# Router scores from a difference of logits on VectorE, one load of the first tokens, and eight fewer waits

## The chip, the cores and the metric

The kernel runs on one core of a Trainium2 chip. The core has five engines with a queue of instructions each: PE (TensorE, matmuls and transposes), DVE (VectorE), ACT (ScalarE), POOL (GpSimd) and SP (SyncE, which here only issues DMAs). Each engine works through its own queue in order and waits at semaphores for the others. The metric is device time in microseconds (us), the median over several executions.

## The reference

The block takes x of shape (4, 1024, 512), thus 4096 tokens of 512 channels. It normalises them with a scale and shift from a conditioning vector, applies a state-space layer of 16 states, adds that to x, normalises again, and adds a mixture of 8 experts. All experts are computed for every token; the router gives 2 of them a score and the other 6 zero.

```python
h = _layernorm(x) * (1 + ca) + sa
x = x + ga * attn(h)          # conv of 4 taps, projections, softplus, scan
h = _layernorm(x) * (1 + cb) + sb
x = x + gb * ffn(h)

# attn: h_t = deltaA_t * h_(t-1) + deltaBu_t, y_t = sum over 16 states of h_t * C_t
# ffn:
logits = jnp.tanh(xt @ Wg1.T) @ Wg2.T              # tokens x 8
_, top_idx = jax.lax.top_k(logits, 2)
top_scores = softmax(take_along_axis(logits, top_idx, axis=1), axis=1)
scores = zeros.at[rows, top_idx].set(top_scores)
up = einsum('td,ehd->teh', xt, Wup) + bup
down = einsum('teh,eoh->teo', silu(up), Wdown) + bdown
out = einsum('te,teo->to', scores, down)
```

With the two largest logits m0 >= m1 of a token, the two scores are 1/(1 + exp(m1 - m0)) and exp(m1 - m0)/(1 + exp(m1 - m0)).

## The kernel before

The 4096 tokens are cut into 8 chunks c of 512. Channels lie on the 128 partitions in 4 tiles. A chunk has 64 scan units (16 states times 4 channel tiles) of 128x512 elements, and each unit goes over four engines:

- ACT writes exp(delta * A) to PSUM (`da`, L996).
- POOL multiplies delta*u by a row of B (`dbu`, L796; DB <- DU, BR).
- DVE runs the scan (`scan`, L1210) into H.
- PE transposes H to tokens x channels in PSUM (`flip`, L1431), and DVE multiplies that by C and adds it to ACC (`acc`, L1235).

The expert layer works on half chunks cs of 256 tokens, 0 to 15. While chunk c is scanned, the two half chunks of chunk c-1 go through the router and the experts: PE multiplies upwards (`up`, L1480 to L1482), ACT applies tanh (`th`, L1098) and a multiply (`t1`, L1103), DVE multiplies by the token's score (`ys`, L1284), POOL makes the product G (`g`, L819), and PE multiplies downwards (`dn`, L1510). At the same time the attention part of the next chunk is prepared: convolution (`conv` on DVE, L1177; `cva` on POOL), projections, softplus, and at the end `del` and `du` on POOL (L760) and `ud` on ACT (L983).

The router of a half chunk is a chain of small steps. PE makes the logits; DVE copies them to LG (L1241), takes the 8 sorted maxima of both halves of 128 tokens into MX (`r3`, L1247) and their indices into IX (`r31`, L1254). ACT then makes PE1 = exp(MX1 - MX0) with one activation for each column (`e1`, L1060) and P0 = PE1 + 1 (L1063). DVE takes P1 = 1/P0 (`r41`, L1257) and P2 = PE1 * P1 (`r42`, L1261). POOL casts the indices from integers to floats, IXF (`r4`, L782), and spreads the two scores over the 8 experts (`sel1` and `sel2` in `select`, L537 to L549); for half chunks 14 and 15 DVE does the latter. PE transposes the result (`r5`, L1467), and through DRAM it comes back as the tile SR that `ys` reads. All steps on DVE here count one semaphore, rt.

The order of the work is written out by hand. `schedule()` makes one list of all tasks of all engines. Each scan unit has two places, numbered over a chunk from 0 to 127, and tables say at which place a task stands: ATTENTION, ROUTER (with a row for each kind of half chunk: "even", "odd", "final", "last", "split"), and PAIR and others for the experts. Each engine walks the list and issues the tasks that are its own. So a table sets only the order within each engine's queue, and semaphores do the rest. In ROUTER a half chunk of the kind "even" has its maxima at place 33 and the scores at 35 to 39 of a chunk, and one of the kind "odd" at 94 to 101.

At the start, SP issues the loads (`begin`, L558 to L567). The first chunk of x comes in two DMAs of 256 tokens, each with its own semaphore (d_xh, d_x). DVE takes the statistics (`sta`, L1166, L1168), POOL the scale (L712 to L718), ACT applies it (`xn`, L898), and PE transposes (`tr`, L1382) after it has made rows of the modulation (L1309). SP waits for the second half of the weight block WM0 (d_wmh) before it issues the loads of AN (A_log) and of WM2.

The weights of the upward product are split into a high part (`whi`, ACT L1018) and a low part (`wlo`, POOL L777, 16 instructions, during chunk 0). A `wlo` issued after the 12th convolution step waits for the convolution step that stands ahead of it in the list.

Of the kernel before, what the change touches and what calls it, by code (L numbers as in the profile page):

```python
# [65 lines left out]
             "r31": 33, "e1": 35, "r4": 38, "r41": 35, "r42": 38, "sel1": 39, "sel2": 39, "r5": 40,  # L66
# [3 lines left out]
             "r31": 96, "e1": 97, "r4": 100, "r41": 98, "r42": 99, "sel1": 101, "sel2": 101, "r5": 101,  # L70
# [3 lines left out]
             "r31": 96, "e1": 97, "r4": 99, "r41": 100, "r42": 100, "sel1": 103, "sel2": 103, "r5": 107,  # L74
# [3 lines left out]
             "r31": 66, "e1": 67, "r4": 69, "r41": 71, "r42": 74, "sel1": 70, "sel2": 76, "r5": 79,  # L78
# [3 lines left out]
             "r31": -18, "e1": -16, "r4": -16, "r41": -15, "r42": -14, "sel1": -14, "sel2": -14,  # L82
# [229 lines left out]
def adaln_kernel(nc, x, pvec, alog, ct, wmod, xpT, dtT, wg1T, wg2T, wupT, bup, wdT, bdn, out):  # L312
    f32, f32r, u32 = mybir.dt.float32, mybir.dt.float32r, mybir.dt.uint32
    ALU, ACT = mybir.AluOpType, mybir.ActivationFunctionType
    EPS = 1e-5
    ctx = ExitStack()
    with ctx:  # L317
# [209 lines left out]
        def select(eng, what, cs):  # L527

            if what == "sel1":
# [4 lines left out]
                eng.wait_ge(S["ixf"], cs + 1)  # L534
                eng.wait_ge(S["rt"], 6 * cs + 5)
# [3 lines left out]
            else:  # L539
                eng.wait_ge(S["rt"], 6 * cs + 6)  # L540
# [13 lines left out]
        def _(eng):  # L554
            for task in order:
                what, *k = task
                if what == "begin":
# [994 lines left out]
```

## Time and profile before

| | |
|---|---|
| Median of 3 runs | 1410.06 us (1409.54 to 1411.26) |
| The profiled execution | 1411.26 us, span of the records 1409.5 us |
| PE (matmul) busy | 1328.6 us, 94% of the span |
| DVE busy | 1222.1 us, 87% |
| POOL busy | 1138.8 us, 81% |
| ACT busy | 987.0 us, 70% |
| Reciprocals L1257 of half chunks 4 and 6 | start at 523.74 and 681.97 us |

A share is taken over the whole span. DVE, POOL and PE all come close to full use in parts of it, so which of them is waited for changes from place to place, and the shares alone don't tell it. A row of a timeline gives an instruction's start, its duration and, in brackets, how long its engine stood idle before it and what that idle time ended with. The time in which one and the same router step comes round again, 158.2 us, is the time of a chunk.

### The profile page before, as it was taken

Reading aid. Unit: us, or ns where it says so; the run is one execution under the profiler, and the core shown is the slowest. Engines: PE = TensorE matmul, PEld = TensorE weight load, DVE = VectorE, ACT = ScalarE, POOL = GpSimd, SP = SyncE. Lnnn points to the kernel's source line nnn. Section 1 sums busy time; section 2 is a strip of 40 time slices with the busy share of each in tenths; the row PEclk is TensorE's granted clock in tenths of the full one; section 3 lists DMA queues with packets and bytes.
Section 4 is the critical chain, followed back from the end, with each engine's and each line's share of the span. In section 5 each row is a group of like instructions: output and inputs, shape, how many; then the busy total and the mean of one; then the engine's idle time right before and its main releaser. Section 6 shows DMA issues by size and latency. Waiting matters only on the chain. (4 is left out here: it accounts for less than half of the span.)

```text
span 1409.5 us, 23418 instructions
## 1 busy us (share of the span) xinstructions
PE 1328.6 (94%) x7500; PEld 956.8 (68%) x7500; DVE 1222.1 (87%) x1725; ACT 987.0 (70%) x2076; POOL 1138.8 (81%) x1173
## 2 busy tenths in 40 slices
PE   8888768999999999999999999999999999999998
PEld 4466645667766776667766776767766767777897
DVE  4799999889897999889997999789998999897554
ACT  4875787588857796588857796588847675656554
POOL 1699889799996989899996989799996978873332
PEclk9899777999999999999999999999999999999999
DMA  6442112334242433534342433434332334433342
GB/s 207 165 151 62 60 38 89 97 96 150 88 136 83 150 120 101 140 97 150 93 132 89 147 117 104 139 94 150 98 131 87 127 105 118 131 90 106 128 134 65
DMA packets 99282, 160.91 MB, mean 114 GB/s; under 512 B 9276, under 2 KB 33980, under 8 KB 99160
## 3 DMA queue, kind: packets, MB, share of 16 engines
q1 hardware_dynamic: 99160, 159.42, 36.5%
q8 instruction: 60, 0.98, 0.3%
q14 instruction: 62, 0.51, 0.1%
HBM read 150.60 MB, written 8.79 MB: 113 GB/s over the span
## 5 line engine op out<-in xcount | busy, mean ns | idle before, releaser
L796 POOL TENSOR_TENSOR DB<-DU,BR 128x512 f32<-128x512 f32 x448 | 579.1, 1309 | 44.7 <-DVE H L1210 23.2
L1235 DVE SCALAR_TENSOR_TENSOR ACC<-pb,CTM,ACC 128x512 f32<-128x512 f32 x512 | 374.9, 733 | 56.0 <-PE pb L1431 54.7
L1510 PE MATMUL pb<-WD,G 128*128 128x512 f32 x856 | 405.1, 593 | 0.0
L996 ACT ACTIVATE pb<-DELP,AN 128x512 f32<-128x512 f32 x448 | 307.2, 686 | 133.5 <-DVE H L1210 131.4
L1431 PEld LDWEIGHTS pb<-ID,H 128*128 128x128 f32 x2048 | 246.9, 144 | 147.8 <-issue 97.6
L1431 PE MATMUL pb<-ID,H 128*128 128x128 f32 x2048 | 316.3, 281 | 26.1 <-DVE ACC L1235 22.0
L1480 PE MATMUL pb<-H2H,WUH 128*128 128x256 f32 x1024 | 314.1, 307 | 13.4 <-DVE TY L1284 12.9
L1210 DVE TENSOR_TENSOR_SCAN H<-pb,DB 128x512 f32<-128x512 f32 x256 | 309.9, 1212 | 15.1 <-ACT pb L996 12.1
L819 POOL TENSOR_TENSOR G<-TY 128x256 f32<-128x256 f32 x256 | 192.0, 753 | 145.2 <-DVE TY L1284 101.2
L1482 PE MATMUL pb<-H2H,WUL 128*128 128x256 f32 x1024 | 289.7, 283 | 0.0
L1481 PE MATMUL pb<-H2L,WUH 128*128 128x256 f32 x1024 | 289.5, 283 | 0.0
L1210 DVE TENSOR_TENSOR_SCAN H<-pb,ST,DB 128x512 f32<-128x512 f32 x192 | 244.4, 1273 | 8.5 <-ACT pb L996 6.6
L1510 PEld LDWEIGHTS pb<-WD,G 128*128 128x128 f32 x856 | 149.0, 190 | 111.9 <-issue 111.0
L1480 PEld LDWEIGHTS pb<-H2H,WUH 128*128 128x128 f32 x1024 | 195.5, 191 | 37.6 <-issue 25.6
L1481 PEld LDWEIGHTS pb<-H2L,WUH 128*128 128x128 f32 x1024 | 196.1, 192 | 4.8 <-issue 4.3
L1482 PEld LDWEIGHTS pb<-H2H,WUL 128*128 128x128 f32 x1024 | 195.5, 191 | 0.0
L1098 ACT ACTIVATE TY<-pb,BUPH 128x256 f32<-128x256 f32 x256 | 106.8, 468 | 123.5 <-PE pb L1482 120.9
L1284 DVE SCALAR_TENSOR_TENSOR TY<-pb,BUP,SR 128x256 f32<-128x256 f32 x256 | 111.1, 474 | 38.5 <-ACT TY L1098 29.8
L1103 ACT ACTIVATE TY<-TY 128x256 f32<-128x256 f32 x256 | 102.5, 413 | 0.0
L1215 DVE TENSOR_TENSOR_SCAN H<-pb,ST,DB 128x256 f32<-128x256 f32 x128 | 88.4, 732 | 2.6 <-ACT pb L1001 1.9
L799 POOL TENSOR_TENSOR DB<-DU,BR 128x512 f32<-128x512 f32 x64 | 81.7, 1287 | 1.7 <-DVE H L1215 1.6
L1332 PE MATMUL pb<-H2H 128*128 128x256 f32 x292 | 58.6, 333 | 3.2 <-ACT H2H L846 3.2
(199 smaller groups left out, 1681.3 us busy)
## 6 DMA issues: line engine op xcount, KB each, us to landing
WD<-in_wdT SPq DMA_DIRECT2D x128, 512.0 KB, 5.0
BR<-bscr SPq DMA_DIRECT2D x112, 256.0 KB, 3.9
SR<-sscr SPq DMA_DIRECT2D x128, 128.0 KB, 4.2
ACC<-in_x SPq DMA_DIRECT2D x16, 512.0 KB, 3.8
out<-ACC SPq DMA_DIRECT2D x32, 256.0 KB, 2.2
DU<-in_x SPq DMA_DIRECT2D x7, 1024.0 KB, 6.5
BR<-bscr SPq DMA_DIRECT2D x32, 128.0 KB, 3.1
DU<-in_xpT SPq DMA_DIRECT2D x8, 320.0 KB, 3.1
```

The lines of the kernel that those rows point to most:

```text
L796: eng.tensor_tensor(DB[:, i % NDB], DU[:, c % 2, r], BR[:, n % 2], ALU.mult).then_inc(S["dbu"], 1)
L819: eng.tensor_tensor(G[:, i % NG], TH[:, m % 2], YS[:, m % 2], ALU.mult).then_inc(S["g"], 1)
L996: eng.activation(DA[i % NDA][:], DEL[:, c % 2, r], ACT.Exp, scale=AN[:, r, n:n + 1]).then_inc(S["da"], 1)
L1098: eng.activation(TH[:, m % 2], up_of(cs, m), ACT.Tanh, scale=0.5, bias=BUPH[:, m:m + 1]).then_inc(S["th"], 1)
L1210: eng.tensor_tensor_scan(H[:, (c * NS + n) % NH, r], DA[i % NDA][:], DB[:, i % NDB], ST[:, n, r:r + 1] if state_from(c, h) else 0.0, ALU.mult,
L1235: eng.scalar_tensor_tensor(out=acc, in0=banks[bank_of["flip", c, n, r]][:], scalar=1.0 if n < 0 else CTM[:, c % 2, j, st:st + 1], in1=acc, ...
L1284: eng.scalar_tensor_tensor(out=YS[:, m % 2], in0=up_of(cs, m), scalar=BUP[:, m:m + 1], in1=SR[:, m // 2 % 2], op0=ALU.add, op1=ALU.mult).t ...
L1431: t = eng.transpose(b[:, dt * 128:dt * 128 + 128], src[:, dt, r * 128:r * 128 + 128], ID[:])
L1480: eng.matmul(b, WUH[:, kk, sl], H2H[:, cs % 2, kk], start=kk == 0, stop=False)
L1481: eng.matmul(b, WUH[:, kk, sl], H2L[:, cs % 2, kk], start=False, stop=False)
L1482: t = eng.matmul(b, WUL[:, kk, sl], H2H[:, cs % 2, kk], start=False, stop=kk == 3)
L1510: eng.matmul(DN[j][:], G[:, (cs * NM + m) % NG, j * 128:j * 128 + 128], WD[:, (cs * NE + m // 2) % NWD, m % 2], start=False, stop=m == NM ...
```

## The change

It has three parts.

1. The router. DVE now makes DM = MX1 - MX0 (a new instruction, ahead of the indices), and ACT one exponential of both columns of DM where it made two, and no copy. DVE adds 1 (the new task `r40`, a tensor_scalar) and takes the reciprocal in place. The cast of the indices moves from POOL to DVE, and the table ROUTER puts it right behind the indices. The semaphores p0 and ixf are gone; rt counts 9 steps for each half chunk instead of 6.
2. The first loads. The first chunk of x comes in one DMA of 1 MB, and the statistics wait for all of it. SP no longer waits for d_wmh before the loads of AN and WM2.
3. The low part of the weights. The `wlo` tasks on POOL no longer wait for the convolution.

In numbers of instructions: DVE has 48 more (3 for each of 16 half chunks), ACT 32 fewer, POOL 16 fewer, SP one DMA fewer; 7 waits of `wlo` go. PE's are the same, in the same order.

```diff
 ROUTER = {
     "even": {...
-             "r31": 33, "e1": 35, "r4": 38, "r41": 35, "r42": 38, ...
+             "r31": 33, "e1": 35, "r4": 33, "r40": 34, "r41": 35, "r42": 38, ...
...
-        PE1, P0, P1, P2 = [RS[:, i] for i in range(4)]
+        DM, PE1, P1, P2 = [RS[:, i] for i in range(4)]
...                                                   # select, sel1
-                eng.wait_ge(S["ixf"], cs + 1)
-                eng.wait_ge(S["rt"], 6 * cs + 5)
+                eng.wait_ge(S["rt"], 9 * cs + 8)
...                                                   # SP, begin
-                    eng.dma_start(DU[:, 0, 0:2], x_v[0][:, 0:2]).then_inc(S["d_xh"], 16)
-                    eng.dma_start(DU[:, 0, 2:4], x_v[0][:, 2:4]).then_inc(S["d_x"], 16)
+                    eng.dma_start(DU[:, 0], x_v[0]).then_inc(S["d_x"], 16)
...
-                    eng.wait_ge(S["d_wmh"], 16)
...                                                   # POOL
-                    taps = [nth[t] for t in order[:at[task]] if t[0] == "conv"]
-                    if taps and taps[-1] > 12:
-                        eng.wait_ge(S["conv"], taps[-1])
...
-                elif what == "r4":
-                    cs = k[0]
-                    eng.wait_ge(S["rt"], 6 * cs + 4)
-                    eng.tensor_copy(IXF[:], IX[:]).then_inc(S["ixf"], 1)
...                                                   # ACT
-                    eng.wait_ge(S["rt"], 6 * cs + 2)
-                    for j in range(2):
-                        eng.activation(PE1[:, j:j + 1], MX[:, j, 0:1], ACT.Exp, scale=-1.0,
-                                       bias=MX[:, j, 1:2]).then_inc(S["e1"], 1)
-                    eng.wait_ge(S["e1"], 2 * (cs + 1))
-                    eng.activation(P0, PE1, ACT.Copy, bias=1.0).then_inc(S["p0"], 1)
+                    eng.wait_ge(S["rt"], 9 * cs + 3)
+                    eng.activation(PE1, DM, ACT.Exp).then_inc(S["e1"], 1)
...                                                   # DVE, sta of chunk 0
-                    if j % 2 == 0:
-                        eng.wait_ge(S["d_x" if j else "d_xh"], 16)
+                    if j == 0:
+                        eng.wait_ge(S["d_x"], 16)
...                                                   # DVE, router
-                    eng.wait_ge(S["rt"], 6 * cs + 2)
-                    if cs:
-                        eng.wait_ge(S["ixf"], cs)
+                    eng.wait_ge(S["rt"], 9 * cs + 2)
+                    eng.tensor_tensor(DM, MX[:, :, 1], MX[:, :, 0], ALU.subtract).then_inc(S["rt"], 1)
                     for j in range(2):
                         eng.max_index(IX[:, j], MX[:, j], LG[:, j]).then_inc(S["rt"], 1)
+                elif what == "r4":
+                    cs = k[0]
+                    eng.wait_ge(S["rt"], 9 * cs + 5)
+                    eng.tensor_copy(IXF[:], IX[:]).then_inc(S["rt"], 1)
+                elif what == "r40":
+                    cs = k[0]
+                    eng.wait_ge(S["e1"], cs + 1)
+                    eng.tensor_scalar(P1, PE1, 1.0, None, ALU.add).then_inc(S["rt"], 1)
                 elif what == "r41":
-                    eng.wait_ge(S["p0"], k[0] + 1)
-                    eng.reciprocal(P1, P0).then_inc(S["rt"], 1)
+                    eng.wait_ge(S["rt"], 9 * k[0] + 7)
+                    eng.reciprocal(P1, P1).then_inc(S["rt"], 1)
```

On DVE, around the maxima of half chunk 0 (kind "even"), this stands in a row before. `H<-pb,ST,DB` is a scan, `ACC<-pb,CTM,ACC` an `acc`; MX, IX, IXF and RS are the router's tiles, and RS holds DM, PE1, P1 and P2.

```order
L1235 SCALAR_TENSOR_TENSOR ACC<-pb2,CTM,ACC 128x512
L1247 MAX MX<-LG 128x8 x2
L1254 MAX_INDEX IX<-MX,LG 128x8 x2
L1210 SCALAR_TENSOR_TENSOR H<-pb1,ST,DB 128x512
L1235 SCALAR_TENSOR_TENSOR ACC<-pb4,CTM,ACC 128x512
L1257 RECIPROCAL RS<-RS 128x2
L1210 SCALAR_TENSOR_TENSOR H<-pb0,ST,DB 128x512
```

And now, in the same place:

```order
L1221 SCALAR_TENSOR_TENSOR ACC<-pb2,CTM,ACC 128x512
L1233 MAX MX<-LG 128x8 x2
L1237 TENSOR_TENSOR RS<-MX 128x2
L1239 MAX_INDEX IX<-MX,LG 128x8 x2
L1243 CAST IXF<-IX 128x16
L1196 SCALAR_TENSOR_TENSOR H<-pb1,ST,DB 128x512
L1247 TENSOR_SCALAR RS<-RS 128x2
L1221 SCALAR_TENSOR_TENSOR ACC<-pb4,CTM,ACC 128x512
L1250 RECIPROCAL RS<-RS 128x2
L1196 SCALAR_TENSOR_TENSOR H<-pb0,ST,DB 128x512
```

The difference and the cast stand ahead of the next scan, and the addition between that scan and the next `acc`.

On DVE, at the indices of half chunk 1 (kind "odd"), before:

```order
L1254 MAX_INDEX IX<-MX,LG 128x8 x2
L1235 SCALAR_TENSOR_TENSOR ACC<-pb3,CTM,ACC 128x512
L1210 SCALAR_TENSOR_TENSOR H<-pb1,ST,DB 128x512
L1257 RECIPROCAL RS<-RS 128x2
L1235 SCALAR_TENSOR_TENSOR ACC<-pb3,CTM,ACC 128x512
L1261 TENSOR_TENSOR RS<-RS 128x2
```

And now:

```order
L1237 TENSOR_TENSOR RS<-MX 128x2
L1239 MAX_INDEX IX<-MX,LG 128x8 x2
L1243 CAST IXF<-IX 128x16
L1221 SCALAR_TENSOR_TENSOR ACC<-pb3,CTM,ACC 128x512
L1196 SCALAR_TENSOR_TENSOR H<-pb1,ST,DB 128x512
L1247 TENSOR_SCALAR RS<-RS 128x2
L1250 RECIPROCAL RS<-RS 128x2
L1221 SCALAR_TENSOR_TENSOR ACC<-pb3,CTM,ACC 128x512
L1254 TENSOR_TENSOR RS<-RS 128x2
```

Here one `acc` and one scan stand between the cast and the addition, and the reciprocal follows the addition at once.

## Rows read from the trace of the kernel before

**Rows 1.** Three stretches: length, busy PE, PEld, DVE, ACT, POOL, clock, DMA, GB/s.

```profile
50.00:225.00 175.00, 135.95 (x752) 100.00 (x752) 167.93 (x196) 135.22 (x246) 157.65 (x144) 0.83 0.26 81
575.00:750.00 175.00, 171.94 (x971) 121.00 (x970) 155.66 (x210) 123.22 (x257) 154.10 (x158) 1.00 0.39 120
1290.00:1409.00 119.00, 110.87 (x690) 97.70 (x688) 64.11 (x114) 65.33 (x163) 41.81 (x49) 0.99 0.32 104
```

**Rows 2.** Timeline of DVE near 32 us: start, duration, instruction, times, idle before it.

```profile
32.62 0.18 DVE L1113 TENSOR_TENSOR MOD<-H 128x16 f32<-128x16 f32 x1
```

**Rows 3.** Timeline of DVE near 53 us.

```profile
52.04 1.19 DVE L1111 TENSOR_SCALAR GBC<-GBC 128x16 f32<-128x16 f32 x1
53.27 1.20 DVE L1113 TENSOR_TENSOR GBC<-GBC 128x16 f32<-128x16 f32 x1
```

**Rows 4.** Timeline of POOL in the same stretch (three instructions, printed as one row).

```profile
50.70 3.73 POOL L796 TENSOR_TENSOR DB<-DU,BR 128x512 f32<-128x512 f32 x3
```

**Rows 5.** Timeline of DVE near 521 us, half chunk 4.

```profile
521.31 0.22 DVE L1247 MAX8 MX<-LG 128x8 f32<-128x8 f32 x2
...
521.86 1.26 DVE L1210 TENSOR_TENSOR_SCAN H<-pb,ST,DB 128x512 f32<-128x512 f32 x1
```

**Rows 6.** Timeline of POOL in the same stretch.

```profile
521.17 0.74 POOL L819 TENSOR_TENSOR G<-TY 128x256 f32<-128x256 f32 x1
521.96 2.52 POOL L767 TENSOR_TENSOR H2L<-XT,H2H 128x512 fp32r<-128x512 f32 x2
```

**Rows 7.** Timeline of ACT near 606 us, half chunk 5.

```profile
605.84 0.47 ACT L1060 ACTIVATE RS<-MX 128x1 f32<-128x1 f32 x2
```

**Rows 8.** Timeline of DVE in the same stretch.

```profile
603.81 0.75 DVE L1235 SCALAR_TENSOR_TENSOR ACC<-pb,CTM,ACC 128x512 f32<-128x512 f32 x1
...
606.58 0.17 DVE L1257 RECIPROCAL RS<-RS 128x2 f32<-128x2 f32 x1 [0.83 <-ACT RS L1063]
```

**Rows 9.** Timeline of POOL in the same stretch.

```profile
604.05 0.73 POOL L819 TENSOR_TENSOR G<-TY 128x256 f32<-128x256 f32 x1
...
606.96 1.43 POOL L537 TENSOR_SCALAR S<-IO,IXF,RS 128x104 f32<-128x104 f32 x2 [0.80 <-DVE RS L1257]
```

**Rows 10.** Timeline of DVE from 684 to 702 us, the rows with idle time.

```profile
686.14 1.22 DVE L1210 TENSOR_TENSOR_SCAN H<-pb,DB 128x512 f32<-128x512 f32 x1 [0.26 <-ACT pb L996]
...
690.98 0.75 DVE L1235 SCALAR_TENSOR_TENSOR ACC<-pb,CTM,ACC 128x512 f32<-128x512 f32 x1 [0.39 <-PE pb L1431]
...
697.39 1.23 DVE L1210 TENSOR_TENSOR_SCAN H<-pb,DB 128x512 f32<-128x512 f32 x1 [0.68 <-POOL DB L796]
```

**Rows 11.** Timeline of DVE from 529 to 540 us, the rows with idle time.

```profile
532.75 0.75 DVE L1235 SCALAR_TENSOR_TENSOR ACC<-pb,CTM,ACC 128x512 f32<-128x512 f32 x1 [0.37 <-PE pb L1431]
...
539.07 1.28 DVE L1210 TENSOR_TENSOR_SCAN H<-pb,ST,DB 128x512 f32<-128x512 f32 x1 [0.56 <-issue]
```

**Rows 12.** Timeline of DVE near 622 us.

```profile
622.50 1.28 DVE L1210 TENSOR_TENSOR_SCAN H<-pb,ST,DB 128x512 f32<-128x512 f32 x1 [2.11 <-ACT pb L996]
```

**Rows 13.** Timeline of PE near 625 us.

```profile
625.35 0.35 PE L1480 MATMUL pb<-H2H,WUH 128*128 128x256 f32 x1 [1.45 <-DVE TY L1284]
```

**Rows 14.** Timeline of PE near 211 us.

```profile
210.75 1.34 PE L1431 MATMUL pb<-ID,H 128*128 128x128 f32 x8 [1.38 <-DVE ACC L1235]
```

**Rows 15.** Timeline of POOL near 95 us.

```profile
94.62 1.26 POOL L777 TENSOR_TENSOR WUL<-XT,WUH 128x512 fp32r<-128x512 f32 x1 [0.69 <-DVE U L1177]
```

**Rows 16.** Timeline of DVE near 5 us.

```profile
5.34 0.69 DVE L1166 BATCH_NORM_STATS2 NA<-DU 128x6 f32<-128x512 f32 x1 [2.18 <-DMA DU<-in_x]
```

**Rows 17.** DMA issues of x, median us from issue to landing.

```profile
DU<-in_x SPq DMA_DIRECT2D x7, 1024.0 KB, 6.5
...
DU<-in_x SPq DMA_DIRECT2D x2, 512.0 KB, 4.6
```

**Rows 18.** Timeline of ACT near 11 us.

```profile
10.80 2.92 ACT L898 ACTIVATE DU<-DU,NA 128x512 f32<-128x512 f32 x4 [1.43 <-POOL NA L718]
```

**Rows 19.** Timeline of PE near 17 us.

```profile
16.59 0.66 PE L1382 MATMUL pb<-ID,DU 128*128 128x128 f32 x4
```

More of the change, by code:

```diff
@@ L65 @@
              "fev": (21, 25), "hh": 32, "hl": (35, 35), "r1": 26, "r12": 29, "r2": 28, "r22": 31, "r3": 33,
-             "r31": 33, "e1": 35, "r4": 38, "r41": 35, "r42": 38, "sel1": 39, "sel2": 39, "r5": 40,
+             "r31": 33, "e1": 35, "r4": 33, "r40": 34, "r41": 35, "r42": 38, "sel1": 39, "sel2": 39, "r5": 40,
              "r52": 43, "sw": 43},
@@ L69 @@
              "fev": (48, 52), "hh": 61, "hl": (65, 74), "r1": 82, "r12": 84, "r2": 89, "r22": 91, "r3": 94,
-             "r31": 96, "e1": 97, "r4": 100, "r41": 98, "r42": 99, "sel1": 101, "sel2": 101, "r5": 101,
+             "r31": 96, "e1": 97, "r4": 96, "r40": 98, "r41": 98, "r42": 99, "sel1": 101, "sel2": 101, "r5": 101,
              "r52": 104, "sw": 104},
@@ L73 @@
              "fev": (46, 49), "hh": 58, "hl": (57, 70), "r1": 81, "r12": 86, "r2": 89, "r22": 84, "r3": 96,
-             "r31": 96, "e1": 97, "r4": 99, "r41": 100, "r42": 100, "sel1": 103, "sel2": 103, "r5": 107,
+             "r31": 96, "e1": 97, "r4": 98, "r40": 100, "r41": 100, "r42": 100, "sel1": 103, "sel2": 103, "r5": 107,
              "r52": 106, "sw": 106},
@@ L77 @@
              "fev": (47, 50), "hh": 55, "hl": (52, 60), "r1": 55, "r12": 56, "r2": 60, "r22": 61, "r3": 66,
-             "r31": 66, "e1": 67, "r4": 69, "r41": 71, "r42": 74, "sel1": 70, "sel2": 76, "r5": 79,
+             "r31": 66, "e1": 67, "r4": 69, "r40": 69, "r41": 71, "r42": 74, "sel1": 70, "sel2": 76, "r5": 79,
              "r52": 79, "sw": 79},
@@ L81 @@
              "fev": (-34, -30), "hh": -23, "hl": (-25, -22), "r1": -24, "r12": -23, "r2": -20, "r22": -20, "r3": -19,
-             "r31": -18, "e1": -16, "r4": -16, "r41": -15, "r42": -14, "sel1": -14, "sel2": -14,
+             "r31": -18, "e1": -16, "r4": -17, "r40": -15, "r41": -15, "r42": -14, "sel1": -14, "sel2": -14,
              "r5": -9, "r52": -10, "sw": -8}}
@@ L435, in adaln_kernel @@
                      "du", "ud", "ug", "da", "dbu", "scan", "st", "flip", "acc", "asm", "ang", "asq", "fsm", "fng", "fsq", "frs", "fxn", "ftr", "fev",
-                     "hh", "hl", "g1", "tg", "g2", "lg", "rt", "sel", "bdz", "bdh", "bdl", "e1", "p0", "ixf", "r5", "stt", "up", "th", "ys", "t1", "g", "bm",
+                     "hh", "hl", "g1", "tg", "g2", "lg", "rt", "sel", "bdz", "bdh", "bdl", "e1", "r5", "stt", "up", "th", "ys", "t1", "g", "bm",
                      "dn0", "dn1", "to", "fin",
-                     "wh", "wl", "gh", "gl", "d_ctx", "d_x", "d_pv", "d_alog", "d_wm0", "d_wmh", "d_xh", "d_wm1", "d_wm2", "d_wm3", "d_wm4", "d_wm5", "d_wg1",
+                     "wh", "wl", "gh", "gl", "d_ctx", "d_x", "d_pv", "d_alog", "d_wm0", "d_wmh", "d_wm1", "d_wm2", "d_wm3", "d_wm4", "d_wm5", "d_wg1",
                      "d_wg2", "d_bup", "d_bdn", "d_xa0", "d_xa1", "d_xp", "d_dtp", "d_bw", "d_br0", "d_br1", "d_gs",
@@ L539, in select @@
             else:
-                eng.wait_ge(S["rt"], 6 * cs + 6)
+                eng.wait_ge(S["rt"], 9 * cs + 9)
                 for j in range(2):
@@ L1249, in _ @@
                     cs = k[0]
-                    eng.wait_ge(S["rt"], 6 * cs + 2)
-                    if cs:
-                        eng.wait_ge(S["ixf"], cs)
+                    eng.wait_ge(S["rt"], 9 * cs + 2)
+                    eng.tensor_tensor(DM, MX[:, :, 1], MX[:, :, 0], ALU.subtract).then_inc(S["rt"], 1)
                     for j in range(2):
                         eng.max_index(IX[:, j], MX[:, j], LG[:, j]).then_inc(S["rt"], 1)
+                elif what == "r4":
[6 more added lines that the diff above has]
+                    eng.tensor_scalar(P1, PE1, 1.0, None, ALU.add).then_inc(S["rt"], 1)
                 elif what == "r41":
-                    eng.wait_ge(S["p0"], k[0] + 1)
-                    eng.reciprocal(P1, P0).then_inc(S["rt"], 1)
+                    eng.wait_ge(S["rt"], 9 * k[0] + 7)
+                    eng.reciprocal(P1, P1).then_inc(S["rt"], 1)
                 elif what == "r42":
                     cs = k[0]
-                    eng.wait_ge(S["rt"], 6 * cs + 5)
+                    eng.wait_ge(S["rt"], 9 * cs + 8)
                     eng.tensor_tensor(P2, PE1, P1, ALU.mult).then_inc(S["rt"], 1)
```

## The prediction

> **What bounds the kernel now.** I read the busy times by stretch first. In a middle stretch of 175 us PE is busy for 171.94, DVE for 155.66 and POOL for 154.10 at a full granted clock; in 50 to 225 us DVE leads with 167.93 and PE has 135.95; in the last 119 us DVE is down to about half [rows 1]. So early in the kernel a microsecond more on DVE counts in full, in the middle PE sets the pace and a late DVE counts where its own idle gaps don't make it up, and at the end it hardly counts.
>
> Then the timelines at the router. After a router step of the even kind DVE has small gaps: in one pattern (half chunks 2, 6, 10) 0.26, 0.39 and 0.68 us [rows 10], in the other (4, 8) 0.37 and 0.56 us [rows 11]. In the odd kind the router is itself on the path. DVE stands 0.83 us before the reciprocal, for ACT's addition [rows 8]; six such waits, of half chunks 1 to 11, repeat this one; POOL stands 0.80 us for that reciprocal before it can spread the scores [rows 9]. Behind that POOL works without a gap to the products `du` of the next chunk, ACT waits for those, DVE then stands 2.11 us for ACT's exponential [rows 12], and PE 1.45 us for DVE's `ys` [rows 13]. That is the one place of a middle chunk at which PE, the bound, stands long; what moves the odd reciprocal moves it.
>
> **The router on DVE: what one small instruction costs.** Three are added for each half chunk. With POOL idle, an instruction of this size takes 0.18 us [rows 2], and starts follow each other at about 0.21: 48 of them would be 10 us of DVE, 0.63 for a half chunk. But the same chain of instructions, run a second time while POOL does its 128x512 products, took 1.19 for a tensor_scalar and 1.20 for a tensor_tensor on 16 columns [rows 3], and each ended where one of POOL's three products, 1.24 apiece, ended [rows 4]. So such a small one is held until the running POOL instruction is over. The maxima and indices are not held: beside POOL's G and H2L [rows 6], max and both indices are through in 0.55, from 521.31 to the scan at 521.86 [rows 5]. No row shows an integer cast on DVE beside POOL. Its bounds are 0.18 [rows 2] and the whole of one POOL product, 1.26 [rows 6]. I take the long one, since the nearest row in form (one input, one output, both in SBUF) is the tensor_scalar of 1.19 [rows 3]; the other end stays for the range.
>
> The Trainium skill bears on this value ("SBUF — State Buffer", section "Who interferes with whom"): copy, cast and tensor_scalar between SBUF tiles can run in modes that take the port pair shared with GpSimd, which is locked for a whole instruction by whoever comes first, and a tensor_tensor with two SBUF inputs contends with a GpSimd instruction that reads SBUF. The trace agrees for the two forms that it shows, 1.19 and 1.20 [rows 3]; by the rule the cast is held too, and by the unheld value instead the sum below would fall to the second rival's.
>
> **Even kind.** Laid on the timeline of half chunk 4: max ends at 521.53. The difference is held until G ends at 521.91, so it costs 0.4 instead of 0.2. The indices take 0.3, to 522.25. The cast is held to the end of the first of the two H2L products, 521.96 + 1.26 = 523.22 [rows 6]. The scan starts at 523.25, not 521.86 [rows 5]: +1.4. The addition stands behind this scan; ACT's exponential is long ready, and the scan ends near the end of the second H2L (524.48 [rows 6]), so I take it at 0.15 (bounds: 0.15 and 1.2, the tensor_scalar of [rows 3]). Together DVE is 1.55 late. In half chunk 0 the same laying gives 1.3 + 0.15 = 1.45.
>
> What becomes of it: half chunk 0 lies where PE waits for DVE at once, 1.38 us [rows 14], so all 1.45 count. In 2, 6 and 10 the gaps of [rows 10] give 1.33 back, leaving 0.22 each, 0.66. In 4 and 8 those of [rows 11] give 0.93 back, leaving 0.62 each, 1.24. Half chunk 12 and later ones I take at nothing: DVE is half idle there [rows 1]. Even kind: 1.45 + 0.66 + 1.24 = 3.35 us.
>
> **Odd kind.** Half chunk 5: the `acc` at 603.81 [rows 8] followed the indices, which take 0.3, so these began at 603.5. The difference is now there and held until POOL's product before G ends, at 604.05 [rows 9]; indices to 604.4; the cast is held to the end of G, 604.05 + 0.73 = 604.78 [rows 9]. An `acc` of 0.75 and a scan of 1.28 [rows 11] end at 606.8, the addition at 607.0, and the reciprocal begins there instead of at 606.58 [rows 8]: +0.4. ACT is no longer waited for: one exponential of the two that took 0.47 together [rows 7] ends near 606.1. So the wait of 0.83 goes, and DVE's own queue, held twice, is late in its place. Behind the reciprocal stand P2 and POOL's scores, and by the chain above the 0.4 goes on to PE. 6 such half chunks (1 to 11): 2.4 us. Half chunk 13 and the last: nothing.
>
> **Relief.** ACT loses one exponential and one copy for each half chunk, some 0.43 us. ACT is busy for 123.22 of 175 us [rows 1] and mostly waits for the scans, so I take nothing. POOL loses the cast, but stood waiting right behind it in the odd kind [rows 9]: nothing. The indices' wait for the cast of the half chunk before was long fulfilled.
>
> **The waits of `wlo`.** Only one was waited out: POOL stood 0.69 us for the convolution [rows 15], in a stretch where DVE needs POOL's products soon after. I take -0.3, between -0.7 (all of it) and +1.3 (that POOL product now starts beside the convolution and holds it once more, by one product of 1.26 as in [rows 15]).
>
> **The first loads.** DVE's statistics begin at 5.34, when the first half of x is there [rows 16]. A half took 4.6 us to land in the median, a whole chunk in later places 6.5 [rows 17]; so they begin up to 1.9 later. ACT's normalisation then ends at 13.72 + 1.9 = 15.6 [rows 18], and PE takes it up at 16.59 [rows 19], behind rows of the modulation. Cost 0, cover left 1.0 us. AN and WM2 are issued earlier behind the same loads and are not waited for early: 0 (bounds 0 and, if they slow the loads that PE waits for, +1).
>
> **Sum.** 3.35 + 2.4 - 0.3 = +5.45. The profiled execution took 1411.26 us (span 1409.5, 1.8 around it), so it becomes 1416.7; it stood 1.2 above the median, 1410.06, so the median becomes **1415.5**. Differences within 0.2%, 2.8 us, can't be told from no change.
>
> **Rivals.**
> 1. The lateness isn't given back. DVE's gaps [rows 10, 11] may only move with the work, because they end on PE and POOL, which DVE itself made late. Then the even kind costs 1.45 + 5 x 1.55 = 9.2, the odd 2.4: +11.3, 1421.4; with the addition held in some, 1423. For it: in 50 to 225 us DVE has 7 us to spare [rows 1]; against: the middle chunks are PE's. Chance 0.12.
> 2. The cast and the additions are not held, or only where it doesn't matter. 0.63 for a half chunk disappears in the gaps of 0.93 to 1.33, half chunk 0 costs 0.6, and the odd reciprocal comes at 603.81 [rows 8] + 0.42 + 0.75 + 1.28 + 0.2 = 606.5, 0.1 early: 0.6 - 0.6 - 0.3, so 1409.8. For it: no row shows the cast itself. Chance 0.25.
> 3. Faster. The holds fall short, and the odd chain, ACT to DVE to POOL to ACT to PE, shortens. The exponential is ready at 606.1 instead of the sum at 606.55, so 0.45 is the most that a reciprocal can come earlier: 6 x 0.45 + 0.7 of `wlo` + 0.3 of ACT in half chunk 0 = -3.7, 1406.4. It decides from where the difference and cast together cost DVE under 0.5 us in the odd kind, since DVE had 0.83 to spare [rows 8]. For it: that slack; against: [rows 3]. Chance 0.16.
> 4. The granted clock, 0.83 in the mean of 50 to 225 [rows 1], stays low for longer since PE has still more gaps there: 4 to 8 us more at half clock where PE is full cost 2 to 4 more, 1417.5 to 1419.5. With the first loads reaching the path, chance 0.05.
>
> The forecast itself has 0.42. Its own range is 1412.9 to 1418.5. Leaving out most of rival 3 (0.12) and the far part of rival 1 (0.07) gives 1408.0 to 1423.0. Faster is rival 3, 0.16; same is rival 2, 0.25; slower is the rest, 0.59.
>
> **What would show it.** Right: the cast lasts about 1 us in the even kind and 0.4 in the odd, the difference 0.4 to 0.6; the scan behind the even indices comes 1.4 later after max; no idle before the odd reciprocals, and POOL's wait for them at about 1.2; a chunk of about 159 us; first statistics near 6.7 to 7.2 with `tr` still near 16.6. Wrong: casts of 0.2 beside POOL products (rival 2); odd reciprocals earlier against their scans (rival 3); gaps behind the even kind as large as before and a chunk of 160 us (rival 1); a low clock past 230 us (rival 4).

## The result and the profile after

The changed kernel is slower. Its median is 1421.76 us over 6 runs (1417.25 to 1424.52); the kernel before took 1411.05 us in the same comparison (6 runs, 1409.54 to 1412.31). The ratio is 1.0075, with a 95% interval of 1.0056 to 1.0094, or 10.7 us. I had forecast +5.5 us, a time of 1415.5 and a range of 1408.0 to 1423.0. The direction and the mechanism (small DVE instructions held by POOL's products) were right, and the forecast size was half of what was measured. The single runs of the changed kernel lie 7.3 us apart, those of the kernel before 2.8.

The profiled execution of the changed kernel took 1423.32 us (span 1421.5), so it is one of its slower ones: 12.1 us above the profiled execution before.

The same stretches as in [rows 1], of the changed kernel. The columns are length, busy PE, PEld, DVE, ACT and POOL, clock, DMA share and GB/s:

```profile
50.00:225.00 175.00, 136.66 (x748) 99.27 (x748) 169.15 (x195) 130.40 (x238) 153.65 (x141) 0.83 0.24 78
575.00:750.00 175.00, 171.73 (x967) 120.47 (x966) 159.18 (x216) 121.36 (x249) 156.60 (x157) 1.00 0.40 123
1290.00:1409.00 119.00, 116.51 (x747) 103.84 (x746) 72.98 (x133) 70.11 (x175) 40.62 (x48) 1.00 0.37 113
```

In the middle stretch PE is as busy as before and DVE has 3.5 us more; the last stretch is shifted by 13 us against the work and compares with nothing. These rows tell little of the loss. The router's own instructions tell more. On the timelines the columns are start, duration, instruction, times and idle time before it. DVE at half chunk 4, where before max, indices and the scan followed each other within 0.55 us [rows 5]:

```profile
524.14 0.23 DVE L1233 MAX8 MX<-LG 128x8 f32<-128x8 f32 x2
524.40 0.35 DVE L1237 TENSOR_TENSOR RS<-MX 128x2 f32<-128x2 f32 x1
...
525.07 1.03 DVE L1243 CAST IXF<-IX 128x16 f32<-128x16 uint32 x1
526.02 1.27 DVE L1196 TENSOR_TENSOR_SCAN H<-pb,ST,DB 128x512 f32<-128x512 f32 x1
527.21 0.14 DVE L1247 TENSOR_SCALAR RS<-RS 128x2 f32<-128x2 f32 x1
```

The difference (L1237) takes 0.35 us, the cast (L1243) 1.03, and the scan starts 1.88 after max instead of 0.55: +1.33. The addition (L1247) takes 0.14. Half chunk 5 on DVE and on POOL, for [rows 8] and [rows 9]:

```profile
606.26 0.57 DVE L1237 TENSOR_TENSOR RS<-MX 128x2 f32<-128x2 f32 x1
...
607.15 0.38 DVE L1243 CAST IXF<-IX 128x16 f32<-128x16 uint32 x1
...
609.47 0.17 DVE L1250 RECIPROCAL RS<-RS 128x2 f32<-128x2 f32 x1
```

```profile
605.53 1.28 POOL L786 TENSOR_TENSOR DB<-DU,BR 128x512 f32<-128x512 f32 x1
606.76 0.74 POOL L809 TENSOR_TENSOR G<-TY 128x256 f32<-128x256 f32 x1
...
609.81 0.73 POOL L536 TENSOR_SCALAR S<-IO,IXF,RS 128x104 f32<-128x104 f32 x1 [1.08 <-DVE RS L1250]
```

The difference ends with POOL's product (606.83 and 606.81), and the cast about with G (607.53 and 607.50). The reciprocal no longer waits, and POOL waits 1.08 us for it where it waited 0.80.

To see where lateness comes and stays I took each PE matmul's start in one trace minus the start of the same matmul before (they stand in the same order in both). Columns are places on the time axis of the kernel before; half chunk 0 lies between 155 and 240 us, 2 to 8 up to 900, 12 between 1140 and 1190, 13 up to 1215, 14 up to 1275. Each row is one execution, with its time in the last column (before: 1411.26).

| kernel | 155 | 240 | 345 | 820 | 900 | 1140 | 1190 | 1215 | 1275 | 1400 | time |
|---|---|---|---|---|---|---|---|---|---|---|---|
| changed | 1.7 | 3.7 | 2.7 | 3.1 | 4.7 | 4.9 | 7.3 | 11.1 | 13.2 | 13.2 | 1423.32 |
| router alone | 0.1 | 0.9 | 0.3 | 1.3 | 2.8 | 3.0 | 5.4 | 5.6 | 7.6 | 7.6 | 1417.79 |
| old router from 12 on | 0.0 | 2.4 | 1.6 | 1.7 | 3.2 | 3.2 | 2.6 | 2.6 | 2.6 | 2.5 | 1412.71 |
| 19 waits on POOL | 1.8 | 3.1 | 3.4 | 7.0 | 7.3 | 9.7 | 9.3 | 9.3 | 10.2 | 10.2 | 1420.43 |
| 13 waits on POOL | 1.1 | 2.3 | 1.4 | 1.5 | 1.8 | 2.2 | 2.1 | 2.1 | 3.1 | 3.1 | 1413.35 |
| no difference on DVE | 3.4 | 5.9 | 4.9 | 4.6 | 5.0 | 5.0 | 7.4 | 7.6 | 9.0 | 9.0 | 1419.18 |
| old router, no `wlo` waits | 1.9 | 2.9 | 1.9 | 1.6 | 1.6 | 1.3 | 1.5 | 1.5 | 1.4 | 1.4 | 1411.71 |

(The step of -1 us between 240 and 345 is in most rows, also of kernels without the new router, so it belongs to the execution before. The changed kernel's last DMA wait was 1.1 us shorter, which is why 13.2 became 12.1.)

So of 13.2 us, 8.3 come in half chunks 12 to 14, which I had put at nothing, 2.0 in half chunk 0, and 1.7 before that, in chunk 0. The first columns are within what executions differ: seven of the kernels below run the same instructions and waits as the kernel before up to the first router step near 208 us, and their profiles lie -0.1 to 3.4 us late at 155. DVE and POOL at half chunk 13 of the changed kernel:

```profile
1202.53 0.21 DVE L1233 MAX8 MX<-LG 128x8 f32<-128x8 f32 x2
1202.77 3.58 DVE L1237 TENSOR_TENSOR RS<-MX 128x2 f32<-128x2 f32 x1
...
1209.93 1.11 DVE L1243 CAST IXF<-IX 128x16 f32<-128x16 uint32 x1
```

```profile
1202.55 2.55 POOL L789 TENSOR_TENSOR DB<-DU,BR 128x512 f32<-128x512 f32 x2
1205.05 1.28 POOL L814 TENSOR_TENSOR ACC<-ACC,XT 128x512 f32<-128x512 f32 x1
```

The difference of 2 columns takes 3.58 us. It waits out three of POOL's products, 1202.55 to 1206.33, not one. That happened in three of the five profiles of this and the later kernels that have the difference and no wait of POOL ahead of it (3.55 to 3.58 us); in the other two it took 1.09. PE before and after at half chunk 12, and after at 13:

```profile
1165.00 0.43 PE L1467 MATMUL pb<-ID,S 128*104 128x128 f32 x2 [1.07 <-POOL S L549]
```

```profile
1171.02 0.43 PE L1460 MATMUL pb<-ID,S 128*104 128x128 f32 x2 [2.21 <-POOL S L548]
```

```profile
1209.41 0.39 PE L1473 MATMUL pb<-H2H,WUH 128*128 128x256 f32 x1 [1.41 <-DVE TY L1277]
```

PE stood for POOL's scores there even before, 1.07 us, so what the router loses goes straight to PE: now 2.21. The clock adds to it. These are the stretches after the two gaps, first before and then after:

```profile
1165.00:1185.00 20.00, 19.58 (x116) 13.90 (x117) 17.77 (x30) 14.22 (x36) 15.08 (x15) 1.00 0.45 126
1200.00:1220.00 20.00, 20.00 (x119) 14.74 (x117) 17.85 (x32) 11.36 (x30) 18.22 (x23) 1.00 0.46 131
```

```profile
1165.00:1185.00 20.00, 17.62 (x98) 13.38 (x97) 19.35 (x33) 13.37 (x35) 15.74 (x19) 0.91 0.34 98
1200.00:1220.00 20.00, 18.28 (x99) 13.33 (x98) 19.33 (x35) 7.96 (x22) 15.00 (x16) 0.91 0.45 133
```

The granted clock is 0.91 in the mean there instead of 1.00: in each of the two, 3.4 us were granted at half, from 1172.5 and from 1210.1 us on (0.09 x 20 us is 1.8 us short of full speed, within rounding half of 3.4). Before, none was from 230 us to the last 3 us. By that the two cost at most 3.4 us of matmul time, an estimate: half of 3.4 us each.

And the convolution step near 91 us, before and after:

```profile
91.53 2.95 DVE L1177 SCALAR_TENSOR_TENSOR U<-DELP,PV,U 128x512 f32<-128x512 f32 x1
```

```profile
90.77 6.11 DVE L1163 SCALAR_TENSOR_TENSOR U<-DELP,PV,U 128x512 f32<-128x512 f32 x1
```

```profile
87.65 3.78 POOL L786 TENSOR_TENSOR DB<-DU,BR 128x512 f32<-128x512 f32 x3
91.38 1.29 POOL L771 TENSOR_TENSOR WUL<-XT,WUH 128x512 fp32r<-128x512 f32 x1
...
96.96 1.26 POOL L740 TENSOR_TENSOR U<-U,DU 128x512 f32<-128x512 f32 x1 [0.63 <-DVE U L1163]
```

Free it takes 0.72 us. Before, it was held until POOL came to the `wlo` that waited for it [rows 15]; in this execution, without that wait, it was held through five products, until POOL stood for it at L740.

### The profile page after: what moved, and what is told of

Read it like the earlier page. It is cut to its first block and busy times, and to the rows that moved or that the text cites. A ratio compares the mean times of both kernels' runs of the same rounds, so it can differ in the third digit from the quotient of the medians.

```text
span 1421.5 us, 23395 instructions
## 1 busy us (share of the span) xinstructions
PE 1335.9 (94%) x7500; PEld 959.8 (68%) x7500; DVE 1251.3 (88%) x1773; ACT 979.0 (69%) x2044; POOL 1135.9 (80%) x1157
## 5 line engine op out<-in xcount | busy, mean ns | idle before, releaser
L1163 DVE SCALAR_TENSOR_TENSOR U<-DELP,PV,U 128x512 f32<-128x512 f32 x57 | 63.2, 1116 | 2.0 <-ACT U L910 1.8
```

## The experiments

Each kernel was timed in 5 rounds against the kernel before; ratios are given with their 95% intervals. The theory (the port): a small DVE instruction is held while POOL's products run, and that lateness reaches PE. Rivals stand with each run.

**The waits of `wlo` put back.** The changed kernel with

```diff
+                    taps = [nth[t] for t in order[:at[task]] if t[0] == "conv"]
+                    if taps and taps[-1] > 12:
+                        eng.wait_ge(S["conv"], taps[-1])
```

> The changed kernel with the seven waits of wlo for the convolution put back; all else as changed. Theory P (the port): the convolution step that took 6.11 us near 91 us is held as long as POOL runs one product behind the other, and POOL's wait for it was what let it in, so with the waits it takes about 2.95 again and 1.7 us of the 10.7 go (what is left of that lateness at 140 us): about 1.0065 times the kernel before. Rival C (the clock): the early lateness comes from half-clock stretches that fell elsewhere, and the waits are worth nothing or the 0.3 us that I forecast: 1.0075 or a little above, with a convolution step as long as now.

Measured: 1419.23 us (6 runs, 1413.60 to 1423.15), ratio 1.0063 (1.0046 to 1.0080). The convolution step took 3.66 us. That goes with the theory, but the interval overlaps with that of the changed kernel (1.0056 to 1.0094), so on the time the run decides nothing. (The 1.7 us that the expectation puts at 140 us stand in the table at 155.)

**The waits of `wlo` taken away alone.** The kernel before without those three lines.

> The kernel before with only the seven waits of wlo taken away. Theory P: the convolution step near 91 us takes about 6.1 us instead of 2.95, and the kernel is 1.5 to 3 us slower, ratio 1.001 to 1.002. Rival C and my forecast for this part: -0.3 us, ratio 0.9998.

Measured: 1411.59 us against 1410.66, ratio 1.0006 (0.9997 to 1.0015). The step took 6.11 us again, as the theory has it. PE was 2.8 us late at 100 us, 0.4 at 140 and 1.9 at 155, and kernels that have the waits reach that too (1.8 and 3.4 at 155 in the table). In time the interval goes from -0.4 to +2.1 us: it can't tell the loss from zero, nor from the forecast -0.3.

**The first loads as before.** The changed kernel with x in two DMAs and the wait on d_wmh.

> The changed kernel with the first loads as before (x in two halves, the wait of SP). My forecast for this part was 0: ratio to the kernel before unchanged at 1.0075, first transposes of x at 16.6 us in both. Rival: the loads of AN and WM2 issued at 4 us cost something later; then up to 1 us less.

Measured: 1422.04 us, ratio 1.0071 (1.0055 to 1.0087). No difference, as forecast. It has no `wlo` waits, and yet the convolution step took 1.20 us in its profile: the long hold comes in some executions, not in all.

**The new router alone.** The kernel before with the router's part of the diff only.

> The kernel before with the new router only (waits and first loads as before). If the parts add up: 10.7 less 1.7 for the waits, thus +9, ratio 1.0064, with 2.0 of it at half chunk 0 and about 8 in half chunks 12 to 14, where the difference of half chunk 13 took 3.58 us. By my forecast the router alone gives 5.75 us, ratio 1.004, none of it behind half chunk 12.

Measured: 1419.48 us, ratio 1.0067 (1.0054 to 1.0081). The router is nearly the whole effect. In its profile, the fastest of its runs, the difference of half chunk 13 took 1.09 us, and the lateness at the end is 7.6 us instead of 13.2.

**The old router in half chunks 12 to 15.** As the run before, but

```diff
+MODE.update({12: 'old', 13: 'old', 14: 'old', 15: 'old'})
```

> The kernel before with the new router for half chunks 0 to 11 alone; 12 to 15 keep the old one. Lateness of instructions in the trace of the changed kernel puts 8 of its 12 us into half chunks 12 to 14. Theory L (the late half chunks): the ratio falls from 1.0067 (new router everywhere) to 1.002 to 1.003, since 3 to 4 us remain (2 at half chunk 0, the rest in the middle). Rival M (my forecast: the middle chunks carry it, and the late ones nothing): it stays at 1.006.

Measured: 1413.74 us (8 runs, 1412.23 to 1414.79), ratio 1.0022 (1.0011 to 1.0032). 1.0067 - 1.0022 is 0.0045, about 6.3 us, in four half chunks of 16. This is the step of my prediction that failed. The spread of single runs is down to 2.6 us.

**The cast left on POOL.** The new router, with the cast at its old place:

```diff
-                    eng.tensor_copy(IXF[:], IX[:]).then_inc(S["rt"], 1)      # on DVE
+                    eng.tensor_copy(IXF[:], IX[:]).then_inc(S["ixf"], 1)     # on POOL
```

> The kernel before with the new router, but the cast of the indices stays on POOL at its old place. The casts on DVE took 1.02 us in the even kind, 0.38 in the odd and 1.11 in 13 and 14. Theory P (each small instruction is held for the rest of a POOL product): without the casts the even kind loses 0.9 of its lateness and cs 13 and 14 about 1 each; of 9 us about half goes, ratio near 1.003. Rival: the difference alone decides, because it is the one that waits out three products at half chunk 13; ratio 1.005.

Measured: 1417.76 us, ratio 1.0046 (1.0034 to 1.0058). Less than half went, which is nearer to the rival's 1.005 than to the expected 1.003, and the interval still touches that of the router alone. The rows of the small instructions (count, busy us, mean ns, idle) in the changed kernel and in this one:

```profile
L1243 DVE CAST IXF<-IX 128x16 f32<-128x16 uint32 x16 | 11.6, 728 | 0.5
L1237 DVE TENSOR_TENSOR RS<-MX 128x2 f32<-128x2 f32 x16 | 11.5, 718 | 0.3
...
L1247 DVE TENSOR_SCALAR RS<-RS 128x2 f32<-128x2 f32 x16 | 4.7, 291 | 0.0
```

```profile
L1304 DVE TENSOR_TENSOR RS<-MX 128x2 f32<-128x2 f32 x16 | 11.2, 698 | 0.3
L1316 DVE TENSOR_SCALAR RS<-RS 128x2 f32<-128x2 f32 x16 | 10.9, 683 | 0.0
```

The casts' 11.6 us are gone, but the additions take 10.9 instead of 4.7: an instruction that comes earlier meets another POOL product. The price belongs to the meeting, not to the operation. The difference of half chunk 13 took 3.56 us in this profile.

**No difference on DVE.** ACT makes two exponentials from MX as before:

```diff
-                    eng.tensor_tensor(DM, MX[:, :, 1], MX[:, :, 0], ALU.subtract).then_inc(S["rt"], 1)
-                    eng.activation(PE1, DM, ACT.Exp).then_inc(S["e1"], 1)
+                    for j in range(2):
+                        eng.activation(PE1[:, j:j + 1], MX[:, j, 0:1], ACT.Exp, scale=-1.0,
+                                       bias=MX[:, j, 1:2]).then_inc(S["e1"], 1)
```

> The kernel before with the new router, but without the difference DM on DVE: ACT makes two exponentials with scale and bias from MX as before, and the addition, cast and reciprocal are on DVE. Theory P: the 0.35 to 1.1 us of each difference go, and 1.1 or 3.6 at half chunk 13; ratio 1.003 to 1.004. The spread of single runs, 1417 to 1424 with the difference, should shrink to about the 4 us of the kernel before, if it comes from the 1 or 3 products that the difference waits out. Rival: the cast carries it all; ratio stays at 1.006.

Measured: 1417.78 us (5 runs, 1416.15 to 1419.27), ratio 1.0049 (1.0036 to 1.0062). If anything, again a part of it: the ratio is above what I expected, and its interval holds both the 1.004 of the theory and the rival's 1.006. The spread of 3.1 us is as expected, but of 5 runs only. The additions took 7.3 us here and waited 3.5 us for ACT.

**POOL waits once, at half chunk 13.** The new router alone, and ahead of one product on POOL

```diff
+                if task in let_in:        # {("dbu", 7, 9, 0): ("rt", rt0(13) + 3)}
+                    eng.wait_ge(S[let_in[task][0]], let_in[task][1])
```

> The kernel before with the new router, and one wait more: at half chunk 13 POOL's product DB (unit 9,0 of chunk 7) waits for the difference. Theory P: the difference then never takes more than one product, at most 1.3 us, in any execution, and the 2.5 us of the executions in which it took 3.58 are gone: median ratio 1.005 to 1.006, single runs within 1413 to 1419. Rival (DVE is late there for another reason, such as the logits): a difference of 3.6 us in the profile and a ratio as without the wait, 1.0067.

Measured: 1419.80 us (1415.46 to 1420.41), ratio 1.0067 (1.0054 to 1.0080). A miss. The difference took 1.10 us in the profile, but it took 1.09 also without the wait in the router-alone profile. The profiles without the wait show that hold in three of five, so some gain was due; none is to be seen, and an interval of 3.7 us from 5 runs could hide one of 1 to 2 us.

**POOL waits at each router step.** The new router alone, with 19 waits on POOL (the expectation says 18). Seven stand ahead of H2L, for the cast of half chunks 0, 2, to 12; six ahead of G, for the cast of 1, 3, to 11; and six in half chunks 12 to 14, for the additions of 12, 13 and 14, the differences of 13 and 14 and the cast of 14.

> The kernel before with the whole new router and its 48 instructions on DVE, and 18 waits more on POOL: its product behind the difference, the cast or the addition waits until that instruction is done. Nothing is taken off DVE. Theory P (they are held by POOL products that run): the casts fall from 1.02, 0.38 and 1.11 us to about 0.2, DVE is some 5 us less late in all, and the ratio falls from 1.0067 to 1.001 to 1.004; POOL, with about 15% idle, hides most of its waits. Rival (the instructions' own time and DVE's lateness cost it, whatever POOL does, or POOL's new waits cost as much as the holds): ratio 1.006 or more.

Measured: 1420.52 us, ratio 1.0063 (1.0050 to 1.0077). The rival's number, but the rows say why:

```profile
608.42 0.17 DVE L1318 CAST IXF<-IX 128x16 f32<-128x16 uint32 x1
```

```profile
POOL G L872 <- DVE IXF L1318: 27.0, 6, 4.5
...
POOL H2L L820 <- DVE IXF L1318: 5.7, 7, 2.1
```

The casts are down to 0.17 us with nothing else changed than POOL standing still. But in the odd kind I had placed the wait too early: POOL stood up to 4.5 us for the cast, six times, and the lateness grows by about 1 us there each time (3.4 to 9.7 from 345 to 1140 us). Over half chunks 12 to 14 it grows by 0.5 where the router alone has 4.6.

**The same without the six waits of the odd kind.** Thirteen waits are left.

> As the run with 18 more waits on POOL, but without the six in the odd kind, where POOL's product G stood 4.5 us for the cast each time and the kernel got about 1 us later each time. The 13 waits of the even kind and of half chunks 12 to 14 stay; in that run the lateness grew by 0.5 us over half chunks 12 to 14, where the new router alone gave 4.6. Theory P: ratio 1.001 to 1.003, the casts of the even kind 0.17 us, lateness at the end 2 to 4 us, and single runs within about 4 us. Rival (the holds are not what costs the time in the even and late half chunks): 1.006 or more again.

Measured: 1413.62 us (10 runs, 1412.82 to 1415.66), ratio 1.0026 (1.0017 to 1.0036). All 48 new instructions are still on DVE, and 13 waits on POOL take 1.0067 down to 1.0026, about 5.8 of 9.5 us. Half chunk 4 in this kernel, DVE and POOL:

```profile
522.86 0.23 DVE L1304 MAX8 MX<-LG 128x8 f32<-128x8 f32 x2
...
523.80 0.17 DVE L1317 CAST IXF<-IX 128x16 f32<-128x16 uint32 x1
523.88 1.28 DVE L1267 TENSOR_TENSOR_SCAN H<-pb,ST,DB 128x512 f32<-128x512 f32 x1
```

```profile
524.05 2.52 POOL L819 TENSOR_TENSOR H2L<-XT,H2H 128x512 fp32r<-128x512 f32 x2 [0.59 <-DVE IXF L1317]
```

The cast takes 0.17 us where it took 1.03, at a price of 0.59 us on POOL, and the scan starts 1.02 after max, not 1.88. That settles the mechanism: it is the hold, and not the instructions' own time, that costs most of the time. 3.7 us remain; the holds of the odd kind, the instructions' own time and POOL's waits are in them, and no run separates them.

**POOL waits for the convolution step near 91 us.** The kernel before with one wait more, on the product ahead of the `wlo` that waits already:

```diff
+            let_in = {("dbu", 0, 6, 0): ("conv", 13)}
```

> The kernel before with one wait more: POOL's product DB (unit 6,0 of chunk 0) waits for the convolution step near 91 us. Theory P: that step, 2.95 to 6.11 us in other traces, takes at most 1.8, and about 1 us is won at 140 us of the trace: ratio 0.999 to 1.000. Rival: POOL is then late by as much: ratio 1.000 to 1.001.

Measured: 1409.77 us against 1410.53, ratio 0.9995 (0.9986 to 1.0004).

```profile
90.87 1.20 DVE L1232 SCALAR_TENSOR_TENSOR U<-DELP,PV,U 128x512 f32<-128x512 f32 x1
```

The step took 1.20 us instead of 2.95, but not through the wait. POOL never stood for it; the step got in one product earlier by itself, as in the profile of the run with the first loads as before (1.20 us), which has no such wait:

```profile
91.47 1.74 POOL L827 TENSOR_TENSOR WUL<-XT,WUH 128x512 fp32r<-128x512 f32 x1
93.17 1.27 POOL L846 TENSOR_TENSOR DB<-DU,BR 128x512 f32<-128x512 f32 x1
```

In the next run, with the same wait, POOL did stand for it at this product, and the step took 1.71 us:

```profile
93.63 1.28 POOL L846 TENSOR_TENSOR DB<-DU,BR 128x512 f32<-128x512 f32 x1 [0.63 <-DVE U L1232]
```

On the time the run decides nothing.

**A try at a faster version.** The old router but for half chunks 1 to 11 of the odd kind, which have the difference, one exponential and the addition, with the cast on POOL; and the wait of the run before.

> A try at a faster version: the old router, except that half chunks 1, 3, 5, 7, 9 and 11 have the difference and the addition on DVE and one exponential on ACT, with the cast left on POOL; and the wait of the run before this. DVE stood 0.83 us there for ACT's addition. If that slack takes up the difference (0.57 to 0.62 us) and the addition, the reciprocal comes 0.1 to 0.2 earlier six times: ratio 0.998 to 0.9995. If the PE transposes behind it set the time of the next acc anyway, as the trace of the changed kernel has it: 1.000.

Measured: 1409.38 us (11 runs) against 1410.53, ratio 0.9988 (0.9977 to 0.9999). Its median is the lowest of all, 0.1% below the kernel before, but the interval ends just short of no change and overlaps that of the run before, so a gain from the odd kind is not shown. DVE's slack of 0.83 us took up the difference:

```profile
603.20 0.57 DVE L1307 TENSOR_TENSOR RS<-MX 128x2 f32<-128x2 f32 x1
...
605.99 0.17 DVE L1327 RECIPROCAL RS<-RS 128x2 f32<-128x2 f32 x1
606.49 0.75 DVE L1290 SCALAR_TENSOR_TENSOR ACC<-pb,CTM,ACC 128x512 f32<-128x512 f32 x1 [0.33 <-PE pb L1501]
```

The reciprocal comes 2.79 us after the difference began; before, it came 3.1 after the indices began (606.58 [rows 8] less 603.5). The `acc` behind it then stands 0.33 us for PE, so only POOL has the earlier scores.

## Why the prediction was half right

The time, 1421.76, lies in the stated range partly by luck. The forecast's own range ended at 1418.5; the wider one, to 1423.0, took in a part of rival 1, whose 1421.4 comes close, and what rival 1 said did not happen. The term that was missing in the sum is half chunks 12 to 14.

**The price of one small instruction: right.** I took holds to the end of the running POOL product from the clamps [rows 3, 4] and the long value for the cast, which no row showed. It took 1.02 to 1.03 us in the even half chunks 2 to 10 and 0.38 in the odd kind (forecast: about 1 and 0.4), and the scan behind the even indices came 1.33 us later after max (forecast 1.4). The rule of the Trainium skill ("SBUF — State Buffer", "Who interferes with whom") that I weighed for the cast holds here: with POOL busy it took 1.03 us, with POOL standing 0.17. The page has the lock for a whole instruction, of whoever came first; here a DVE instruction also waited out three products (3.58 us) and five (6.11 us), one behind the other, and the measurement decides.

**Half chunks 2 to 10: right in the sum, not in the parts.** Forecast 1.9 us after the gaps gave theirs back, 0.22 or 0.62 for each. The table has 2.2 from 345 to 1140 for the changed kernel, the odd kind included (0.6 to 2.9 in the other profiles with the same router there and no wait of POOL). From half chunk 4 to 6 a chunk took 158.38 us after 158.23 before, where I had written about 159. Of this, 1.6 came at half chunk 8 alone, where PE stood for DVE's `acc`; the profile with 13 waits on POOL has 0.3 there:

```profile
860.29 0.66 PE L1424 MATMUL pb<-ID,H 128*128 128x128 f32 x4 [1.24 <-DVE ACC L1221]
```

The other even ones cost 0.3 at most: between 684.5 and 702 us DVE had no gap left, where it had 1.33 us [rows 10]. Rival 1, that nothing is given back, is out: it has 1.55 for each of five.

**The odd kind: mis-sized, 2.4 forecast, about 0.1 each measured.** The holds came as laid out. But the reciprocal is 0.17 us later against its surroundings, not 0.4 (609.47 - 606.58 is 2.89, and all around is 2.72 late), because instructions start some 0.08 us before the end of the one ahead, which I left out. And the `acc` behind it had waited for PE before, so that P2 is not late at all.

**Half chunk 0: 1.45 forecast, 2.0 measured.** The difference met H2L instead of G and took 1.11 us:

```profile
210.50 1.11 DVE L1237 TENSOR_TENSOR RS<-MX 128x2 f32<-128x2 f32 x1
...
211.93 0.92 DVE L1243 CAST IXF<-IX 128x16 f32<-128x16 uint32 x1
```

In the router-alone profile the same step gives 0.8, and in the three profiles with the old router in half chunk 0 beside the kernel before it gives 1.0, 1.0 and 0.0. Executions differ by as much as the term, so it is neither confirmed nor refuted.

**Half chunks 12 to 14: the step that failed.** The sum had 0 for them, and the trace has 8.3 us. "Half chunk 12 and later ones I take at nothing: DVE is half idle there" rested on the stretch from 1290 us [rows 1]. Half chunks 12 to 14 lie ahead of it. This is the kernel before there:

```profile
1100.00:1290.00 190.00, 186.44 (x1099) 137.65 (x1098) 175.12 (x308) 122.51 (x312) 147.81 (x159) 1.00 0.39 117
```

PE was busy for 186.44 of 190 us, DVE for 175.12. Their router is on PE's path: PE stood 1.07 us for POOL's scores before the change. Here the cast, the addition (1.28) and the difference are held in turn. The run with the old router there puts 6.3 us on them.

**The clock: a rival that I had in the wrong place.** I had a lower clock between 160 and 230 us as a rival. From 50 to 225 us the mean is 0.83 as before. The lower clock came in half chunks 12 and 13, behind PE's longer gaps. Not each such gap brings it: in the profile with the waits of `wlo` put back PE stood 2.21 us at the same place, no half-clock stretch followed, and half chunk 12 cost 1.1 us instead of 2.4. Gaps of 1.68 us before (872.28) and 1.80 after (1278.43) had no half-clock stretch behind them either, so the gap's length alone does not decide.

**The waits of `wlo`: the mechanism wrong, the cost not shown.** Forecast -0.3, bound +1.3. I saw the 0.69 us that POOL stood [rows 15] as a loss. It was what ended a hold of 2.95 us. But whether the longer hold costs time is open. PE was 2.6 us late behind it, at 100 us, and 0.2 at 140; the 1.7 us at 155, and the 1.9 in the run alone, are no more than kernels with the waits have (-0.1 to 3.4), and half-clock stretches fell at other places in each. The ratio of the run alone leaves -0.4 to 2.1 us.

**The first loads: right.** The statistics began 1.34 us later, and the transposes of x on time (16.57, before 16.59 [rows 19]):

```profile
6.68 0.69 DVE L1152 BATCH_NORM_STATS2 NA<-DU 128x6 f32<-128x512 f32 x1 [3.47 <-DMA DU<-in_x]
```

```profile
16.57 0.66 PE L1375 MATMUL pb<-ID,DU 128*128 128x128 f32 x4
```

**What stays open.** The runs show the hold and that POOL's standing still ends it; that a port which both engines share is its cause is argued, and no run tests it apart. Why a DVE instruction gets in at the next boundary between two POOL products in one case and not in another is open too. At half chunk 13 it started 0.22 us after POOL's product both in the changed kernel (3.58 us) and with the waits of `wlo` back (1.09 us). What makes single runs differ by 7 to 10 us is open in part. Half chunks 12 to 14 take part, since without the new router there the spread is 2.6 us, and with 13 waits on POOL 2.8; the three-product hold (half chunk 13 cost 2.6 us with it and without the clock, 0.2 to 0.3 without both) and the clock behind PE's gaps (1.1 to 1.4 us each) explain some 4 us of it.

## What to carry to other kernels

Before moving a small operation to VectorE, look at what GpSimd runs at that moment: 0.2 us of work cost up to 1.3 us here, and 3.6 in three of the profiles. Where such a meeting can't be avoided, a wait on GpSimd for the small instruction, placed just ahead of the product behind it, was the cheaper side (0.59 us once instead of 0.86 on VectorE), and a wait that looks idle may be doing this already. When a stretch is called harmless, read the busy times of exactly that stretch.

## What the runs showed of the hardware

- The same convolution step (128x512, VectorE) takes 0.72 us free. Near 91 us it took 1.20 (twice), 1.7 (four times), 2.9 (twice), 3.7 (four times) and 6.11 us (twice) in fourteen profiles. It ended by itself at a boundary between two GpSimd products, or when GpSimd stood. Where it got in by itself, the GpSimd product beside it took 1.72 to 1.74 us instead of 1.28.
- A VectorE subtraction of 128x2 took 0.14 us with GpSimd idle, 0.23 to 1.12 beside one product, and 3.55 to 3.58 over three. Max, indices and the reciprocal stayed at 0.14 to 0.18 each, beside such products too.
- In six profiles PE stood 2.20 or 2.21 us for the scores of half chunk 12. In four of them a stretch of 3.4 us at half the full clock (1.2 instead of 2.4 GHz) followed, in two it didn't. In the eight profiles with a gap of 1.05 to 1.36 us there it never did. Half chunk 12 cost 1.0 to 1.1 us in the two and 2.3 to 2.4 in the four, so this is one source of the spread of single runs.
